# FP4 rounding of x in the bank of q and k instead of the bank of v, with a new order of all engines

## The reference

```
xn = layernorm(x)
q, k, v = xn Wq', xn Wk', xn Wv'       16 heads of 16; q and k are divided by their norm
s = softmax(q k' + alibi + mask) v     each query sees itself and the 127 keys before it
s = s Wo'
fp4(z): blocks of 16; scale = max|z| / 6; z/scale rounded to 0, .5, 1, 1.5, 2, 3, 4, 6; times scale
gate, up = fp4(xn) fp4(Wg)', fp4(xn) fp4(Wu)'       704 wide
g = silu( fp4(silu(gate) * up) fp4(Wd)' )
out = x + s * g
```

## Time and profile before

| | |
|---|---|
| time, median of 3 executions | 514.56 us (513.56 to 520.21) |
| the profiled execution: time / span | 519.24 us / 517.4 us |
| mean granted clock of TensorE | 0.984 |
| busy: PE, DVE, ACT, POOL | 438.6 (85%), 390.7 (75%), 363.7 (70%), 368.7 us (71%) |
| chain that ended last | PE 56%, DVE 16%, DMA 9%, issue 9%, ACT 6%, POOL 2% |

### The profile page before, as it was taken

One profiled execution on the slowest core, in us unless ns is written; L12 is line 12 of the kernel. 1 busy time (PEld: TensorE's weight loads), 2 busy tenths in 40 slices (PEclk: granted clock), 3 DMA queues, 4 the chain that ended last, 5 costly groups with the idle time before them and its releaser, 6 DMA issues.

```text
span 517.4 us, 21326 instructions
## 1 busy us (share of the span) xinstructions
PE 438.6 (85%) x8612; PEld 308.3 (60%) x8612; DVE 390.7 (75%) x776; ACT 363.7 (70%) x561; POOL 368.7 (71%) x854
## 2 busy tenths in 40 slices
PE   0037887999999899999889899799999999998885
PEld 0015555667666666666666566466666766666664
DVE  4898797887877787887776678578788787775482
ACT  3455798777778677777865677677777777777640
POOL 4756777877777787787776688767777777766071
PEclk9999899999999999999998899899999999999998
DMA  8212156536577755556985666955545764553525
GB/s 297 74 31 63 42 109 98 110 75 151 98 126 122 122 121 110 101 111 107 122 112 89 105 114 89 119 106 122 105 105 99 91 111 103 111 112 62 91 57 111
DMA packets 175010, 54.40 MB, mean 105 GB/s; under 512 B 164224, under 2 KB 174272, under 8 KB 174912
## 3 DMA queue, kind: packets, MB, share of 16 engines
q1 hardware_dynamic: 174480, 52.90, 55.3%
q10 hardware_dynamic: 432, 0.13, 0.1%
HBM read 7.54 MB, written 4.19 MB: 23 GB/s over the span
## 4 chain that ended last, share of the span: by engine, by line
PE 56%; DVE 16%; DMA 9%; issue 9%; ACT 6%; POOL 2%; SPq 0%; DVEq 0%; POOLq 0%; ACTq 0%
PE bank_b L590 13%; PE gt L566 12%; PE up L378 11%; DMA ahT<-ah_stack 7%; PE gt L580 4%; PE bank_b L378 4%; DVE up L828 4%; DVE vals L917 3%; PE scores L523 3%; PE bank_b L384 2%; ACT ffn_gate L1346 2%; DVE bank_b L784 2%; DVE x_grid L791 2%; PE bank_q L378 1%; DMA x_all<-wproj 1%
## 5 line engine op out<-in xcount | busy, mean ns | idle before, releaser
L590 PE MATMUL bank_b<-probs,vals 64*32 64x64 f32 (+1 forms) x3904 | 75.0, 220 | 14.6 <-DVE vals L917 14.2
L1333 ACT ACTIVATE probs<-scores 128x768 f32<-128x768 f32 (+1 forms) x101 | 80.4, 796 | 4.8 <-PE scores L547 4.2
L590 PEld LDWEIGHTS bank_b<-probs,vals 64*32 64x32 f32 (+1 forms) x3904 | 60.6, 108 | 32.6 <-DVE vals L917 17.4
L378 PE MATMUL up<-wgu_hi,xT 128*128 128x352 f16 x248 | 64.7, 327 | 0.0
L378 PE MATMUL gt<-wgu_hi,xT 128*128 128x352 f16 x256 | 62.4, 312 | 1.6 <-ACT wgu_lo L1196 0.9
L378 PE MATMUL bank_q<-wproj_hi,xT 128*128 128x512 f16 x128 | 45.7, 399 | 19.8 <-DMA xT<-x_stack 11.8
L1584 POOL TENSOR_TENSOR ah_stack<-att,ah_stack 128x256 f16<-128x256 f32 x32 | 21.6, 677 | 44.2 <-ACT ah_stack L1196 44.2
L1196 ACT ACTIVATE pv_t<-bank_b 128x512 f32<-128x512 f32 x31 | 18.5, 597 | 47.5 <-PE bank_b L590 47.5
L799 DVE SCALAR_TENSOR_TENSOR up<-up,h_gain,gate 128x704 f32<-128x704 f32 x31 | 29.7, 959 | 28.3 <-PE up L378 27.7
L1196 ACT ACTIVATE qk_stack<-bank_q 128x512 f16<-128x512 f32 x64 | 35.1, 595 | 22.7 <-DVE bank_q L896 22.7
L896 DVE TENSOR_TENSOR bank_q<-bank_q,rsq 128x512 f32<-128x512 f32 x32 | 22.3, 698 | 35.0 <-POOL rsq L1677 35.0
(11 more groups left out here) (235 smaller groups left out, 1349.1 us busy)
## 6 DMA issues: line engine op xcount, KB each, us to landing
out<-y SPq DMA_DIRECT2D x32, 128.0 KB, 2.9
x_all<-x SPq DMA_DIRECT2D x20, 128.0 KB, 3.2
x_all<-x SPq DMA_DIRECT2D x3, 512.0 KB, 4.3
x_all<-wproj SPq DMA_DIRECT2D x1, 768.0 KB, 7.3
dn_raw<-wd SPq DMA_DIRECT2D x1, 704.0 KB, 8.9
probs<-wg SPq DMA_DIRECT2D x1, 640.0 KB, 5.6
probs<-wu SPq DMA_DIRECT2D x1, 640.0 KB, 7.8
xT<-x_stack SPq DMA_TRANSPOSE x34, 3.9
```

Of the source, the lines that this page charges most:

```text
L378: done = e.matmul(out, lhs[i][:, kt, :], rhs[j][:, kt, lo:hi], start=n == 0, stop=n == len(terms) - 1)
L590: done = e.matmul(pv_bank(i)[32 * n:32 * n + 32, grp * P + q:grp * P + q + HB], va, pr, start=first and grp == 0, stop=last and grp == 3)
L1333: e.activation(probs[j % P_BUFS][:, grp, :, window(j)].rearrange("p (b e) w -> p b e w", b=2), score_banks(j, grp)[:, :, :, window(j)], AC ...
```

## The change

The rounding of x (norm_x to grid_x) works in the first 256 columns of bank_q for tiles 4 to 30 instead of in bank_b for tiles 4 to 31. It comes after lo_qk(t), the last reader of q and k of the same tile, and qk_mm(t+1) waits for grid_x(t) instead of for lo_qk(t). v_mm(t) waits for attend(t-4) instead of for grid_x(t). In the loop, DVE, ACT and POOL therefore round tile t in pass t, where before they rounded tile t+1 in pass t. The third load of x is issued behind the transposes x_transpose(0), x_transpose(1) and stack_transpose(0). The order of all five engines is new, at the start, in the loop and at the end. No instruction is added or removed. The core of the diff:

```
         def in_psum(t):
-            return 4 <= t
+            return 4 <= t < LAST
         def x_round(t):
-            return bank_b[:, 0:D] if in_psum(t) else x_ring[:, XN_BUFS + t % 2]
+            return bank_q[:, 0:D] if in_psum(t) else x_ring[:, XN_BUFS + t % 2]
...
# qk_mm
+                elif in_psum(t - 1):
+                    e.wait_ge(s_x_step[GRID], t)
                 else:
                     e.wait_ge(s_lo_qk, t)
# v_mm
-                if in_psum(t):
-                    e.wait_ge(s_x_step[GRID], t + 1)
+                if t >= 4:
+                    e.wait_ge(s_att, t - 3)
# norm_x
                 if in_psum(t):
-                    e.wait_ge(s_att, t - 3)
+                    e.wait_ge(s_lo_qk, t + 1)
# SP, the start
-            e.wait_ge(s_lo_wproj, KT)
-            e.dma_start(*x_group(2)).then_inc(l_x[2], 16)
             x_transpose(0)
             x_transpose(1)
             stack_transpose(0)
+            load_third()
...
```

PE, the loop:

```
             for t in range(4, 31):
                 qk_mm(t)
                 gate_mm(t - 2)
+                v_mm(t)
                 scores(t - 1, 0)
-                v_mm(t)
                 scores(t - 1, 1)
                 pv(t - 3)
                 scores(t - 1, 2)
-                wo_mm(t - 4)
                 up_mm(t - 2)
                 up_mm_last(t - 2)
                 pv_rest(t - 3)
                 scores(t - 1, 3)
                 down_mm(t - 4, 0, 4)
+                wo_mm(t - 4)
+                down_mm(t - 4, 4, FT)
                 back(t - 3)
-                down_mm(t - 4, 4, FT)
```

More of the change, by code:

```diff
@@ L1098, in vector_program @@
+            unit(3)
             hidden(1)
             amax_h(1)
-            up_x(3)
+            lo_qk(3)
             wide_h(1)
-            wide_x(4)
+            lo_wo()
             rscale_h(1)
-            unit(3)
-            grid_x(3)
-            ln_moments(6)
             norm_h(1)
             denom(0)
-            lo_qk(3)
             attend(0)
-            amax_x(5)
-            rscale_x(4)
-            norm_x(4)
-            ln_stats(7)
+            up_x(3)
+            grid_x(3)
@@ L1115, in vector_program @@
+            wide_x(4)
             squares(4)
             up_h(1)
-            up_x(4)
-            grid_x(4)
+            ln_stats(7)
+            values(4)
             grid_h(1)
-            values(4)
             unit(4)
-            ln_moments(7)
             for t in range(4, 31):
+                rscale_x(t)
+                hidden(t - 2)
+                lo_qk(t)
+                if exists(t + 3):
+                    ln_moments(t + 3)
+                norm_x(t)
+                amax_h(t - 2)
+                up_x(t)
+                wide_h(t - 2)
+                grid_x(t)
+                rscale_h(t - 2)
+                norm_h(t - 2)
+                gated(t - 4)
+                denom(t - 3)
+                attend(t - 3)
+                up_h(t - 2)
+                squares(t + 1)
@@ L1124, in vector_program @@
                 if exists(t + 4):
                     ln_stats(t + 4)
-                wide_x(t + 1)
-                rscale_x(t + 1)
-                lo_qk(t)
-                hidden(t - 2)
-                amax_h(t - 2)
-                wide_h(t - 2)
-                rscale_h(t - 2)
-                denom(t - 3)
-                norm_h(t - 2)
-                attend(t - 3)
-                gated(t - 4)
-                norm_x(t + 1)
-                up_h(t - 2)
-                squares(t + 1)
@@ L1411, in scalar_program @@
             hi_wd(0)
+            exp(1, 2)
             hi_wd(1)
-            square_x(2)
             lo_wd(0)
@@ L1416, in scalar_program @@
             hi_k(2)
+            square_x(2)
             square_h(0)
+            exp(1, 3)
+            lo_wd(1)
+            square(3)
             hi_wd(2)
-            lo_wd(1)
-            exp(1, 2)
-            square(3)
+            silu(1)
             hi_xn(4)
-            exp(1, 3)
-            silu(1)
             exp(2, 0)
-            square_x(3)
+            hi_q(3)
+            hi_k(3)
             exp(2, 1)
@@ L1429, in scalar_program @@
             exp(2, 2)
-            hi_q(3)
-            hi_k(3)
             hi_xn(5)
+            square_x(3)
+            exp(2, 3)
             square_h(1)
-            hi_att(0)
-            exp(2, 3)
-            square(4)
             for t in range(4, 31):
-                square_x(t)
+                square(t)
+                hi_att(t - 4)
                 silu(t - 2)
@@ L1694, in gpsimd_program @@
             root(-1, LINEAR)
+            pad_stack(0)
             root(-1, QUAD)
@@ L1773, in gpsimd_program @@
             root(3, ROOT)
+            lo_h(0)
             x_norm(5)
+            hi_h(0)
+            fine_x(3)
             ln_parts(6)
+            lo_xn(5)
             lo_qx(3)
-            lo_h(0)
+            floor_ss(4)
+            coarse_h(1)
             hi_qx(3)
-            lo_att(0)
-            floor_ss(4)
-            lo_xn(5)
             root(4, SEED)
@@ L1784, in gpsimd_program @@
             root(4, ARG)
-            coarse_h(1)
+            lo_att(0)
             root(4, LINEAR)
-            coarse_x(4)
             root(4, QUAD)
```

437 lines of the change are left out of this document (220 added, 217 removed).

## The result

The kernel after took 501.28 us (median of 4 runs, 500.10 to 502.26), the kernel before 517.17 us beside it (4 runs, 513.56 to 520.21). The ratio is 0.9743, with a 95% interval from 0.9708 to 0.9779: faster. The profiled execution took 501.43 us with a span of 499.6, so 1.83 us lie outside it. Against the profiled 519.24 us of before that is 17.8 us less; between the medians it is 15.9. The profiled execution of before was one of its long ones.

What follows compares the result with a forecast made beforehand. TensorE was taken as busy 12.85 of 13.66 us a tile, with late transposes costing 12.0 in the loop. From 519.24, 12.0 late transposes, 1.6 period, 2.5 start and 3 end gave 500.1 us; range 491 to 513.

Steps and rivals of the forecast that it cites:

- Late transposes, 12.0: Loop: wo_mm's waits for the transposed ah and the slower clock around them cost 12.0 us, all of which should go.
- what followed the waits: Loop: what follows wo_mm's late-transpose waits, at a granted clock of 0.89, was said to cost more than the 6.8 us waited.
- The room of 7.0 us: Loop: time given to ah's transpose from issue to its new first reader, down_mm; the longest landing took 6.65 us.
- Period, 13.6: Loop: one undisturbed tile falls from 13.66 to 13.6 us, bounds 13.4 and 13.9; 1.6 us over the loop.
- The ring on bank_b: Loop: attention steps and x's rounding shared bank_b, making v_mm and pv wait 0.22 and 0.59 us; the rounding leaves it.
- half a us to spare: Loop: grid_x lets qk_mm(t+1) go at 13.05 us and PE comes to it at 13.55, leaving 0.5 us.
- Start, 2.5: Before qk_mm(4): the earlier x transpose frees 3.9 us, of which 2.5 were taken; bounds 3.9 and a loss of 2.
- End, 3: After qk_mm(31): the last q and k transpose comes 4.9 us earlier; 3 taken, bounds 5 and a loss of 2.
- GpSimd did not become the bound: Loop: rival that POOL's dependent steps slow and bound the tile at 14.5 us, total 524.4; chance 0.08.
- Only the late transposes go: Whole kernel: rival that waits merely change places (13.75 us a tile) and the ends bring nothing, total 509.7; chance 0.22.
- Transfers late elsewhere: Loop: rival that transfers land late at the scores or qk_mm instead and 12 us stay, total 512; chance 0.10.
- the signs that I had named: New profile: no ahT or v_mm waits, short exp waits, period 13.6; wrong if qk_mm waits over 0.1 us a tile for x_grid.

Runs made afterwards that it cites:

- Run 1: Kernel before with one edit: wo_mm(t-4) issued behind back(t-3) instead of ahead of up_mm(t-2); 508.20 us, ratio 0.983.
- run 4: Kernel after with wo_mm(t-4) put back ahead of up_mm(t-2); 622.49 us, ratio 1.203.
- run 2: Kernel before with x's rounding always in its SBUF buffer, so v_mm no longer waits for grid_x; 512.23 us, ratio 0.990.
- run 8: Kernel after with x's rounding always in its SBUF buffer instead of the PSUM bank of q and k; 500.93 us, ratio 0.966.
- run 5: Kernel before with two edits: wo_mm(t-4) behind back(t-3), and x's rounding in its SBUF buffer; 507.19 us, ratio 0.978.
- run 10: Kernel after with VectorE's lo_qk(31) moved from behind grid_x(31) to behind up_h(29) in the tail; 506.95 us, ratio 0.984.
- run 3: Kernel after with the third load of x issued ahead of the two x transposes again; 504.85 us, ratio 0.977.
- run 11: Kernel before with x's rounding in SBUF and wo_mm, gated, add_x and the store of y one tile later; 505.32 us, ratio 0.980.
- run 6: Kernel before with the third load of x issued behind the first two x transposes and the first stack's; 518.93 us, ratio 1.000.
- the last run: Kernel after's start and tail joined to before's loop orders with x's rounding in SBUF and wo_mm one tile later; 511.00 us, ratio 0.990.

## Why the prediction was right

Predicted were 500.0 us (491 to 513); measured are 501.28. By the profile the sum was 500.1 against 501.43: the start is 0.4 us longer than forecast, the loop 1.6 longer and the end 0.7 shorter.

- **Late transposes, 12.0.** Right. Run 1 took them away alone and the loop lost 11.4. Two readings in the working were loose. Over the five passes, what followed the waits did not cost more than the waits: of the 12.0 us, 6.8 are waits, some 0.6 are the first pass, and the rest is mainly the clock behind the waits. And the first pass is no late transpose: run 1 still has it, at 14.29. The room of 7.0 us was 6.9 (issued at 399.09, read by down_mm at 405.98). It was needed more than I thought: with the landing at 5.8 us in the median, run 4 shows what the old place would cost in the new order.
- **Period, 13.6.** 13.52, within the bounds. The waits came as worked out: pv 0.18 forecast and 0.26 measured, third scores 0.23 and 0.21, up_mm 0.29 and 0.31. lo_qk began 10.03 us after qk_mm (10.07 forecast), the root was over at 7.60 (7.6), and grid_x ended at 12.84 (12.9), ahead of a qk_mm at 13.51. The ring on bank_b was the right cause: run 2 frees it alone and the period falls. That the new bank has half a us to spare was right (0.67), and run 8 shows that the bank isn't needed.
- **What the loop gave back.** Not forecast: 3.8 us over 27 undisturbed passes. The loop was forecast at 367.2 and measured at 368.8. The period won 3.8 instead of 1.6, and 3.8 were lost again; that these nearly cancel is luck, and without the second the forecast of the loop would have been 2.2 us too long. The kernels with the old orders lose 0.5 us in this way (run 1: 369.5 less 27 x 13.67 = 0.4; run 5: 0.5), so it comes with the new order. In after and in run 10, which have the same loop, the same five passes are the long ones (those that end with qk_mm of tiles 16, 17, 20, 21 and 27), and 0.4 to 0.5 us of each is a slow pv_rest; run 3 has the same loop and nearly the same passes, and in runs 1, 5 and 11 pv_rest takes its 1.2 us in all five. The rest is the first pass (1.2) and small delays in three others, less 0.5 us in the pass that is shorter. What slows pv_rest is open; no run was made for it.
- **Start, 2.5.** 2.1, but the working was wrong in kind. I had taken the load's 3.9 us as the gain and the new order as something that could only eat of it; that 2.5 was near 2.1 is luck. The first product did come 4.5 us earlier. Runs 3 and 6 show that each alone brings 0.7 at most by the fifth product, and that the new order is needed to pass the earlier product on to the later ones.
- **End, 3.** 3.7. The step that I had named is one on which the end hangs: run 10 takes it back and pays 5.7. It is not shown to be the whole gain, since the forecast had neither the two table loads that fell away nor the waits for ah at the very end. The transpose was issued 13.2 us after qk_mm(31) and not at 11.3, so it lands only just ahead of scores(31, 0): 462.70 and the median landing of 3.8 make 466.5, and the scores begin at 466.69.
- **Rivals.** GpSimd did not become the bound (root at 7.60). "Only the late transposes go" is what run 1 measured, 508.2, 1.5 below the 509.7 that I had given it. Transfers late elsewhere: 0.7 us in the loop, and 2.3 and 0.4 in the end, where before had 3.6. Of the signs that I had named, qk_mm waited for x_grid once in the loop, 0.4 us in all, and the granted clock from 90 to 445 us is 1.00.

## What to carry to other kernels

Ask of every transfer how long it is given, from issue to the first reader in queue order, and compare that with the longest landing in the trace and not with the typical one; here one line moved across TensorE's queue was worth 9 to 11 us, and putting it back in the new order cost 121. Price a long wait on TensorE by the pass it stands in and not by itself: waits of 1.91 and 3.18 us made their passes 3.6 and 5.7 us longer, since the clock fell behind them. Before you count a moved wait as gained, name the instruction that covered the next one (wo_mm covered the exponents, 0.15 us a pass), and when you splice good parts of two orders, follow the queues of all engines over the seam: both losses of the last run were one instruction in the wrong place of a queue.

## What the runs showed of the hardware

- A TensorE wait of 3.18 us in a loop pass (run 4) was followed by 3.75 us at a granted clock of 0.50, one of 4.12 us (run 10) by 3.64 us at 0.50, and one of 2.00 us (run 3, the end) by 3.08 us at 0.52. Of the shorter waits for the transposed ah, one of 1.10 us in before was followed by 2.17 us at 0.51 and one of 1.91 by 0.50, but the other one of 1.1 in before and the one of 1.66 in run 2 left the clock at 1.00, so the length of the one wait doesn't decide by itself. The waits of 0.2 to 0.3 us, three in a pass of after, left it at 1.00.
- The transpose of ah, from SBUF to SBUF and of one size, landed after 4.2 us in the median in before and after 5.8 in after, with the longest at 6.7 and 6.4. It goes with the order of the loop: all seven kernels with the old one have 4.2 or 4.3 us, all seven with the new one 5.5 to 5.8. The transpose of q and k took between 3.6 and 6.3 us. What in the order decides it, no run here separated.
- A switch of tables took ScalarE 1.28 us (ACT_TABLE_LOAD), 66 times in before and 64 in after, with the same list of steps in another order.
- In the kernel after and in run 10, whose loops are the same, the same five passes have a pv_rest of 1.5 to 1.7 us instead of 1.16, in some of them with idle time of TensorE that no semaphore or transfer in the trace ends (0.26 us at 240.83). Runs 1, 5 and 11, with the old order, have 1.2 us in these passes.
